# The fall-back verdict of a top-k attention kernel: carried to one SBUF row by a transfer instead of summed over the rows by a TensorE matmul

## The chip, the cores and the metric

The kernel runs on one core of one Trainium2 chip. The metric is the device time of one execution in microseconds (us), lower is better. TensorE (PE) multiplies matrices, VectorE (DVE), ScalarE (ACT) and GpSimd (POOL) work elementwise, SyncE (SP) issues all DMA transfers here. Each engine runs its own instructions in program order; engines wait for each other, and for transfers, on semaphores.

## The reference, cut to what matters

Input is one sequence of 2048 rows by 1024 columns in float32. Three layers follow each other: a mixture layer, the attention, and the same mixture layer again. The attention has 32 query heads over 8 key/value heads (four query heads share one), head size 32, and keeps for each query and head only the 204 largest causal scores:

```python
draft = jnp.einsum('bhqd,bhkd->bhqk', qr, kr)
draft = draft + jnp.where(causal_future, neg, jnp.asarray(0.0, dtype))
num_remain = max(min(Sq, MIN_REMAIN), Sq - int(Sq * MASK_OUT))
_, draft_indices = jax.lax.top_k(draft, num_remain)
mask = jnp.full((B, H, Sq, Sq), neg, dtype)
...
scores = jnp.einsum('bhqd,bhkd->bhqk', qr, kr) / np.sqrt(HD).astype(np.float32) + mask
attn = jax.nn.softmax(scores, axis=-1)
out = jnp.einsum('bhqk,bhkd->bhqd', attn, v)
```

## The kernel before, in words

Phase A (to about 828 us) does the first mixture layer and the projections, phase B (828 to 4199 us) the attention, phase C the rest. The change touches phase B alone.

Phase B goes through 128 **places** p. A place is one tile of 128 queries with one key/value group, so four heads. Groups 0, 2, 4, 6 take their tiles 0 to 15 upward, the odd groups 15 to 0 downward. Tile i sees 128*(i+1) keys, so a low tile is narrow and a high one wide. Tile 0 keeps all its keys and is not searched; 120 places are.

For a searched place the kernel looks for each query's threshold. PE computes the scores, DVE copies them to SBUF (`evacuate`, L1121), ACT counts by sign sums how many lie above a guess (L948), POOL improves the guess twice (`first_update`, `second_update`), DVE subtracts it (`difference`, L1129), finds the eight scores nearest to it (`nearest`, L1142, L1144) and picks the exact threshold from them (`choose`, result `dk`). DVE then writes the four masks (`masks`, L1259). PE multiplies keys by queries again with the masks added (`weights`, L834 to L840), ACT takes the exponential (L957), PE multiplies with the values (`values`, L868), turns the result back (`turn_back`, L878), and DVE normalises it (`normalise`, L1265, L1268).

The pick can fail where too many scores lie between guess and threshold. POOL's `judge` therefore makes `bad`, 128 queries by four heads in bf16, non-zero where it failed (L1082 is the last of its seven operations). PE's `flags` (L886) multiplies `bad` by a matrix of ones, which leaves in every row of four PSUM columns the sum over the 128 queries. DVE's `read_flag` (L1159) takes the maximum of the four columns into `flg`, and `fall_back` loads it into a register (L1167) and branches (L1168): if it is above zero, a slow exact search is run on DVE. In this input that happens in four places.

What sets the order: each engine's program is written out by a loop over j, with stages of several places in one turn. In turn j, DVE evacuates place j+2, searches place j (`directions`, `nearest`, `choose`), does `difference` of j+1, `normalise` of j-2, three of the four masks of j, `read_flag(j)`, the fourth mask, `fall_back(j)`, and a small memset (L1298) that counts up the semaphore `go`. PE does in turn j the weights of place j-1, and between them at fixed shares of the row the scores of j+2 and the first of j+3; `flags(j)` stands at the end of the row (share 1.0), or behind `turn_back(j-2)`. The first `weights` of place j in the next turn waits for `go`. POOL does in turn j `selectors(j)`, `second_update(j+1)`, `judge(j)`, `fold(j+1)`, `first_update(j+2)`. SP does in turn j `store(j-2)`, then seven transfers of queries for place j+4.

Of the kernel before, what the change touches and what calls it, by code (L numbers as in the profile page):

```python
# [17 lines left out]
ALU = mybir.AluOpType  # L18
ACT = mybir.ActivationFunctionType
AX = mybir.AxisListType  # L20
# [607 lines left out]
FLAGS = REP * VP  # L628
# [4 lines left out]
FLAG_AT, NEXT_R_AT = 1.0, 0.75  # L633


def phase_b(nc, b, dram):
# [12 lines left out]
    def searching(p):  # L649
        return here(p) and searched[p]  # L650
# [29 lines left out]
    def spread(events, n):  # L680

        at = [[] for _ in range(n + 1)]
        for f, e in events:
            at[math.ceil(f * n) if e[0] == "F" else int(f * n)].append(e)
        return at

    with ExitStack() as ctx:
# [28 lines left out]
        heads_bad = sb("heads_bad", [P, REP])  # L716
        rec = sb("rec", [P, REP])
# [12 lines left out]
        sm = semaphores(nc, ctx, "fill rs evac sign t1 t2 df sel key dk bad flagged flg mask go st ex pv ot otr norm mf "  # L730
# [4 lines left out]
        written = [ctx.enter_context(nc.semaphore(f"b_written{n}")) for n in range(2)]  # L735

# [9 lines left out]
        with nc.Block() as block:  # L746
            @block.sync
            def _(sp):
# [24 lines left out]

                def store(p):
# [11 lines left out]
                for j in range(N + 2):  # L786
                    if j >= 2:
                        store(j - 2)
# [10 lines left out]
            def _(pe):  # L799
# [71 lines left out]
                def turn_back(p):  # L871
# [3 lines left out]
                    if chosen[min(p + 2, N)]:  # L875
                        pe.wait_ge(sm["flg"], chosen[min(p + 2, N)])
# [14 lines left out]
                for j in range(-2, N + 2):  # L891
# [4 lines left out]
                    if searching(j):  # L896
                        events.append((FLAG_AT, ("F", j, 0)))
# [4 lines left out]
                    held = None  # L902
                    for n in range(len(todo) + 1):
                        for kind, p, h in at[n]:
                            if kind == "R":
                                scores(p, h)
                            elif back:
                                flags(p)
                            else:
                                held = p  # L910
# [11 lines left out]
                        if not back and seen == min(LAG + 2, blocks[p]):  # L922
                            turn_back(j - 2)
                            back = True
                            if held is not None:
                                flags(held)
# [72 lines left out]
            def _(pool):  # L999
# [72 lines left out]
                def judge(p):  # L1072
# [9 lines left out]
                    gp.tensor_tensor(bad[:, p % 2, :], c, far, ALU.add).then_inc(sm["bad"], 1)  # L1082
# [15 lines left out]
            def _(dve):  # L1098
# [58 lines left out]
                def read_flag(p):  # L1157
                    dve.wait_ge(sm["flagged"], chosen[p + 1])
                    v.tensor_scalar(heads_bad[:, :], psum[:, 7, FLAGS:FLAGS + REP], 0.0, None, ALU.add, ALU.max,  # L1159
                                    accum_out=flg[:, 0:1]).then_inc(sm["flg"], 1)  # L1160

                def fall_back(p):
# [5 lines left out]
                    with dve.If(any_bad > 0):  # L1168
# [6 lines left out]
                        then(v.tensor_scalar(heads_bad[:, :], heads_bad[:, :], 0.0, None, ALU.is_gt))  # L1175
                        then(v.tensor_reduce(several, heads_bad[:, :], AX.X, ALU.add))
                        then(v.tensor_tensor(heads_bad[:, :], heads_bad[:, :], b.steps[:, 0:REP], ALU.mult))
                        then(v.tensor_reduce(c, heads_bad[:, :], AX.X, ALU.max))
                        then(v.tensor_scalar(which, c, 0.5, None, ALU.subtract))
# [39 lines left out]
                        then(v.tensor_scalar(several, several, 1.5, None, ALU.is_gt))  # L1219
                        then(v.tensor_tensor(c[0:QUAD, :], c[0:QUAD, :], several[0:QUAD, :], ALU.max))  # L1220
# [128 lines left out]
```

## Time and profile before

| | |
|---|---|
| median of three runs | 4733.16 us (4732.83 to 4733.44) |
| the profiled execution: time, span | 4739.29 us, 4737.5 us |
| busy DVE, PE, ACT, POOL, share of the span | 67%, 74%, 57%, 43% |
| mean granted TensorE clock | 0.843 of full speed |
| packets of the DMA queue that SP fills, share of 16 DMA engines | 8.9% |

The span is the profiled execution from first to last instruction. A busy share is a mean over three unlike phases, so it does not say what holds up phase B; the waits do. A wait is put down to the instruction that released it last. For DVE, ACT and POOL the time in which an instruction only waits or branches is idle time of the engine.

### The profile page before, as it was taken

How to read it: one execution, taken by the hardware profiler on the slowest of the kernel's cores; microseconds unless marked ns; L12 is line 12 of the kernel's file. 1: busy time of each engine (PE TensorE's matmuls, PEld its weight loads, DVE VectorE, ACT ScalarE, POOL GpSimd, SP SyncE). 2: the span in 40 equal slices, each digit the busy share in tenths (PEclk: the TensorE clock that was granted, in tenths of full speed). 3: DMA queues.
4: the chain of work that ended last, by engine and by line, in shares of the span. 5: the costliest groups of instructions: out<-in, count | busy, mean ns of one | idle time of the engine just before them, and what ended most of it. 6: DMA issues, size and time to landing. Idle time of an engine off the chain costs nothing. (4 is left out here: it accounts for less than half of the span.)

```text
span 4737.5 us, 56552 instructions
## 1 busy us (share of the span) xinstructions
PE 3524.3 (74%) x16248; PEld 1649.4 (35%) x16248; DVE 3173.2 (67%) x6104; ACT 2688.0 (57%) x4577; POOL 2023.6 (43%) x5916
## 2 busy tenths in 40 slices
PE   5777775677868757787885678888567888857776
PEld 2333332233323323333332233333233333324443
DVE  2444444688988758888884888887488888822222
ACT  0111111688858757886885688887478888820000
POOL 1121211655535755554575554456565445620000
PEclk8777776688989878898997789989779999978887
DMA  2111111100001010000100100010010000011111
GB/s 97 42 52 43 51 40 44 34 11 11 9 6 21 16 30 12 11 9 7 21 16 19 24 11 9 9 21 14 19 26 11 9 9 11 15 72 53 54 40 40
DMA packets 221534, 124.04 MB, mean 26 GB/s; under 512 B 187940, under 2 KB 206628, under 8 KB 221092
## 3 DMA queue, kind: packets, MB, share of 16 engines
q1 hardware_dynamic: 221092, 119.36, 8.9%
q8 instruction: 130, 2.13, 0.2%
q14 instruction: 312, 2.56, 0.2%
HBM read 76.28 MB, written 42.99 MB: 25 GB/s over the span
## 5 line engine op out<-in xcount | busy, mean ns | idle before, releaser
L868 PE MATMUL banks<-pT,v_sb 128*65 128x512 f32 x2176 | 1186.3, 629 | 34.9 <-ACT oT L972 33.4
L957 ACT ACTIVATE pT<-banks 128x512 f32<-128x512 f32 x1088 | 637.7, 592 | 641.3 <-PE banks L840 634.9
L816 PE MATMUL banks<-k_sb,q_sb 128*128 128x512 bf16 (+3 forms) x1280 | 515.5, 403 | 388.5 <-DVE sc L1121 355.0
L1144 DVE MAX8 near<-keys 128x8 f32<-128x256 f32 (+14 forms) x480 | 653.4, 1361 | 16.5
L948 ACT ACTIVATE junk<-sc,t_all 128x256 fp8e4<-128x256 f32 (+14 forms) x480 | 599.2, 1249 | 31.9 <-DVE sc L1121 30.1
L948 ACT ACTIVATE junk<-sc,tiny 128x256 fp8e4<-128x256 f32 (+14 forms) x480 | 595.5, 1246 | 36.5 <-DVE sc L1129 36.2
L948 ACT ACTIVATE junk<-sc,tt 128x256 fp8e4<-128x256 f32 (+14 forms) x480 | 598.4, 1247 | 1.4 <-POOL tt L1013 0.8
L834 PE MATMUL banks<-q_sb,k_sb 128*128 128x512 bf16 x1088 | 447.0, 411 | 146.4 <-DVE fb L1298 124.7
L1121 DVE TENSOR_SCALAR_CACHE_REDUCE sc<-banks 128x1024 f32<-128x1024 f32 (+7 forms) x512 | 501.3, 980 | 52.1 <-PE banks L821 30.0
L1129 DVE TENSOR_SCALAR sc<-sc,tt 128x256 f32<-128x256 f32 (+14 forms) x480 | 360.5, 814 | 241.6 <-POOL tt L1034 241.5
L818 PE MATMUL banks<-k_sb,q_sb 96*128 96x512 bf16 (+3 forms) x1280 | 504.8, 404 | 0.0
L840 PEld LDWEIGHTS banks<-eye,mk 128*128 128x128 bf16 x4352 | 359.9, 103 | 301.2 <-issue 73.3
L840 PE MATMUL banks<-eye,mk 128*128 128x128 bf16 x4352 | 448.6, 228 | 0.0
L836 PE MATMUL banks<-q_sb,k_sb 99*128 99x512 bf16 x1088 | 444.9, 409 | 0.0
L1021 POOL TENSOR_SCALAR pw_b<-dd 128x4 f32<-128x4 f32 x120 | 31.8, 265 | 880.9 <-ACT junk L948 880.9
L1142 DVE TENSOR_SCALAR keys<-sc,flip 128x256 int32<-128x256 int32 (+14 forms) x480 | 393.0, 819 | 5.7 <-issue 1.4
L354 PE MATMUL banks<-wqkv,a_xT 128*128 128x512 f32 x768 | 376.1, 654 | 13.6 <-ACT a_xT L168 13.6
L816 PEld LDWEIGHTS banks<-k_sb,q_sb 128*128 128x128 bf16 x1280 | 138.4, 108 | 665.4 <-DVE sc L1121 455.9
L1259 DVE TENSOR_SCALAR mk<-sc,dk 128x256 bf16<-128x256 f32 (+14 forms) x480 | 369.5, 812 | 0.3 <-issue 0.3
L168 ACT ACTIVATE a_xT<-banks 128x512 f32<-128x512 f32 x64 | 34.7, 594 | 463.0 <-PE banks L148 463.0
L868 PEld LDWEIGHTS banks<-pT,v_sb 128*65 128x65 f32 x2176 | 228.7, 147 | 50.1 <-issue 38.7
L834 PEld LDWEIGHTS banks<-q_sb,k_sb 128*128 128x128 bf16 x1088 | 113.4, 104 | 380.2 <-DVE fb L1298 141.5
(247 smaller groups left out, 5469.8 us busy)
## 6 DMA issues: line engine op xcount, KB each, us to landing
q_sb<-scratch_qk SPq DMA_DIRECT2D x896, 32.0 KB, 1.9
scratch_qk<-parts SPq DMA_DIRECT2D x16, 960.0 KB, 3.7
a_x<-in_x SPq DMA_DIRECT2D x16, 512.0 KB, 3.2
scratch_x<-a_x SPq DMA_DIRECT2D x16, 512.0 KB, 2.6
scratch_attn<-o_sb SPq DMA_DIRECT2D x128, 64.0 KB, 1.6
c_xn<-scratch_attn SPq DMA_DIRECT2D x16, 512.0 KB, 3.6
c_x<-scratch_x SPq DMA_DIRECT2D x16, 512.0 KB, 4.5
out<-c_x SPq DMA_DIRECT2D x16, 512.0 KB, 2.6
```

Source lines behind the costliest of these rows:

```text
L354: last = nc.tensor.matmul(b.psum[:, 4 * (t % 2) + j, :], b.xT[:, t % U, c, :], wqkv[:, c, j * BANK:(j + 1) * BANK], start=(c == 0), stop=( ...
L816: nc.tensor.matmul(r_slot(n)[:, j:j + wj], q_sb[:, p % QS, 0, h, :], k_sb[:, group[p] % 2, 0, col:col + wj], start=True, stop=False)
L818: last = nc.tensor.matmul(r_slot(n)[:, j:j + wj], q_sb[0:K1, p % QS, 1, h, :], k_sb[0:K1, group[p] % 2, 1, col:col + wj], start=False, sto ...
L834: nc.tensor.matmul(psum[:, bank, :], k_sb[:, group[p] % 2, 0, cols], q_sb[:, p % QS, 0, :, :].rearrange("p h n -> p (h n)"), start=True, s ...
L836: nc.tensor.matmul(psum[:, bank, :], k_sb[0:ONES_AT + PARTS_OF_MAX, group[p] % 2, 1, cols], q_sb[0:ONES_AT + PARTS_OF_MAX, p % QS, 1, :, : ...
L840: last = nc.tensor.matmul(psum[:, bank, h * P:(h + 1) * P], mk[:, p % 2, h, cols], b.eye16[:, :], start=False, stop=(h == REP - 1))
L868: nc.tensor.matmul(psum[0:VP, 6, :], v_sb[:, group[p] % 2, kb, :], pT[:, n % PTS, :], start=(kb == 0), stop=(kb == blocks[p] - 1)).then_in ...
L948: nc.scalar.activation(junk[:, n % 2, 0:w], s, ACT.Sign, bias=bias, scale=scale, accum_out=into, saturate=False)\
L957: nc.scalar.activation(pT[:, tn % PTS, :], psum[:, 4 + n % 2, :], ACT.Exp, scale=SCALE)\
L1121: v.tensor_scalar(sc[:, p % SCS, h, c * CHUNK:c * CHUNK + w], r_slot(n)[:, 0:w], 0.0, mx[:, p % 4, 0, h:h + 1] if c else None, ALU.add, AL ...
L1142: link(v.tensor_scalar(z.bitcast(I32), sc[:, p % SCS, h, 0:width[p]].bitcast(I32), 2, flip[:, h:h + 1], ALU.logical_shift_right, ALU.bitwi ...
L1144: v.max(near[:, h, :], z).then_inc(sm["key"], 1)
```

## The change

Five things are changed. PE's `flags` goes, with its place in PE's order and with the wait of `turn_back` on `flg`. SP gets `carry_verdict(j)` as the first thing of turn j: it waits for `bad` and moves the 128x4 bf16 values from 128 SBUF rows into one row of 512 elements (`verdict`, two slots in turn). `read_flag(j)` waits for that transfer's semaphore (`carried`) and takes the maximum over 512 SBUF elements of one row, in place of four PSUM columns. `fall_back` works out which heads failed from `verdict` when the branch is taken, with one more reduction. POOL waits with its next write into the same slot of `bad` until the slot has been carried.

```diff
+                def carry_verdict(p):
+                    sp.wait_ge(sm["bad"], chosen[p + 1])
+                    if p >= 2:
+                        sp.wait_ge(sm["go"], p - 1)
+                    sp.dma_start(verdict[0:1, chosen[p] % 2, :, :], bad[:, chosen[p] % 2, :]).then_inc(carried[chosen[p] % 2], 16)
...
                 for j in range(N + 2):
+                    if searching(j):
+                        carry_verdict(j)
                     if j >= 2:
                         store(j - 2)
...
-                    if chosen[min(p + 2, N)]:
-                        pe.wait_ge(sm["flg"], chosen[min(p + 2, N)])
...
-                def flags(p):
-                    pe.wait_ge(sm["bad"], chosen[p + 1])
-                    if p >= 2:
-                        pe.wait_ge(sm["norm"], p - 1)
-                    nc.tensor.matmul(psum[:, 7, FLAGS:FLAGS + REP], b.ones16[:, :], bad[:, p % 2, :],
-                                     start=True, stop=True).then_inc(sm["flagged"], 1)
...
-                    gp.tensor_tensor(bad[:, p % 2, :], c, far, ALU.add).then_inc(sm["bad"], 1)
+                    if chosen[p] >= 2:
+                        pool.wait_ge(carried[chosen[p] % 2], 16 * (chosen[p] // 2))
+                    gp.tensor_tensor(bad[:, chosen[p] % 2, :], c, far, ALU.add).then_inc(sm["bad"], 1)
...
                 def read_flag(p):
-                    dve.wait_ge(sm["flagged"], chosen[p + 1])
-                    v.tensor_scalar(heads_bad[:, :], psum[:, 7, FLAGS:FLAGS + REP], 0.0, None, ALU.add, ALU.max,
-                                    accum_out=flg[:, 0:1]).then_inc(sm["flg"], 1)
+                    dve.wait_ge(carried[chosen[p] % 2], 16 * (chosen[p] // 2 + 1))
+                    if chosen[p]:
+                        dve.wait_ge(sm["flg"], chosen[p])
+                    v.tensor_scalar(passed[:, :], verdict[:, chosen[p] % 2, :, :].rearrange("o q h -> o (q h)"), 0.0, None,
+                                    ALU.add, ALU.max, accum_out=flg[0:1, 0:1]).then_inc(sm["flg"], 1)
...
-                        then(v.tensor_scalar(heads_bad[:, :], heads_bad[:, :], 0.0, None, ALU.is_gt))
+                        then(v.tensor_reduce(heads_bad[0:1, :], verdict[:, chosen[p] % 2, :, :].rearrange("o q h -> o h q"),
+                                             AX.X, ALU.max))
+                        then(v.tensor_scalar(heads_bad[0:1, :], heads_bad[0:1, :], 0.0, None, ALU.is_gt))
```

How the order on the engines moves is shown at place 36 (group 2, tile 4). On PE, before, at the end of its turn; the names after the arrow are the inputs, L878 turns back place 34, L816 to L821 are scores of place 39, L834 is the first `weights` of place 36:

```order
L868 MATMUL banks<-pT,v_sb 65x512 [waits b_ot,b_ex]
L878 MATMUL banks<-eye,oT 128x65 [waits b_flg,b_norm,b_ot]
L878 MATMUL banks<-eye,oT 128x65 x3
L886 MATMUL banks<-bad,ones 128x4 [waits b_norm,b_bad]
L816 MATMUL banks<-k_sb,q_sb 128x512 [waits b_evac]
L818 MATMUL banks<-k_sb,q_sb 128x512
L816 MATMUL banks<-k_sb,q_sb 128x512
L818 MATMUL banks<-k_sb,q_sb 128x512
L821 MATMUL banks<-future,eye 128x128
L834 MATMUL banks<-q_sb,k_sb 128x512 [waits b_ex,b_go]
```

On PE, now, at the same place; where the changed file's lines L826 to L844 are L816 to L834 before, L878 is L868, and L886 is L878:

```order
L878 MATMUL banks<-pT,v_sb 65x512 [waits b_ot,b_ex]
L886 MATMUL banks<-eye,oT 128x65 [waits b_norm,b_ot]
L886 MATMUL banks<-eye,oT 128x65 x3
L826 MATMUL banks<-k_sb,q_sb 128x512 [waits b_evac]
L828 MATMUL banks<-k_sb,q_sb 128x512
L826 MATMUL banks<-k_sb,q_sb 128x512
L828 MATMUL banks<-k_sb,q_sb 128x512
L831 MATMUL banks<-future,eye 128x128
L844 MATMUL banks<-q_sb,k_sb 128x512 [waits b_ex,b_go]
```

The matmul on `bad` is gone and nothing else has moved; the scores of place 39 no longer stand behind a wait for `bad`, and the `weights` still stand behind `go`.

On DVE, before, around `read_flag` of place 36:

```order
L1268 TENSOR_TENSOR o_sb<-banks,rec 128x128 [waits b_written0,b_vchain]
L1259 TENSOR_SCALAR mk<-sc,dk 128x640 [waits b_dk,b_st]
L1259 TENSOR_SCALAR mk<-sc,dk 128x640 x2
L1159 TENSOR_SCALAR heads_bad,flg<-banks 128x4 [waits b_flagged]
L1259 TENSOR_SCALAR mk<-sc,dk 128x640
L1167 TENSOR_LOAD flg [waits b_flg]
```

On DVE, now, the same place:

```order
L1265 TENSOR_TENSOR o_sb<-banks,rec 128x128 [waits b_written0,b_vchain]
L1256 TENSOR_SCALAR mk<-sc,dk 128x640 [waits b_dk,b_st]
L1256 TENSOR_SCALAR mk<-sc,dk 128x640 x2
L1154 TENSOR_SCALAR passed,flg<-verdict 1x512 [waits b_flg,b_carried1]
L1256 TENSOR_SCALAR mk<-sc,dk 128x640
L1162 TENSOR_LOAD flg [waits b_flg]
```

The place in the order is the same; the wait is now for a transfer, and the fourth mask, the load of the flag and `go` stand behind it as before.

On SP, now, two turns (L780 is the new transfer, L784 the store, L756 the loads of queries; before, the rows were the same without L780):

```order
L780 DMA verdict<-bad 1x128x4 [waits b_go,b_bad]
L784 DMA scratch_attn<-o_sb 128x128 [waits b_norm]
L756 DMA q_sb<-scratch_qk 32x4x128 [waits b_st]
L756 DMA q_sb<-scratch_qk 32x4x128 x6
L780 DMA verdict<-bad 1x128x4 [waits b_go,b_bad]
```

Store and loads of a turn now stand behind the wait for that turn's `bad`.

## Rows read from the trace of the kernel before

**Rows 1.** Windows: phase B; us, busy (instructions) of each engine, clock, DMA.

```profile
828.00:4199.00 3371.00, 2567.82 (x12902) 1134.11 (x12903) 2683.80 (x4980) 2529.36 (x4221) 1855.89 (x5448) 0.87 0.07 15
```

**Rows 2.** Waits of DVE: who for whom, us in total, times, longest.

```profile
DVE sc L1129 <- POOL tt L1034: 241.5, 84, 12.7
...
DVE dirn L1133 <- ACT junk L948: 149.8, 57, 4.8
...
DVE fb L1298 <- issue: 50.1, 20, 3.4
```

**Rows 3.** Waits of PE.

```profile
PE banks L886 <- POOL bad L1082: 237.1, 97, 7.1
...
PE banks L834 <- DVE fb L1298: 124.7, 58, 22.6
```

**Rows 4.** Timeline, place 36 (tile 4): start, us, instruction, [idle before <-releaser].

```profile
1773.75 0.49 POOL L1082 TENSOR_TENSOR bad<-gp,js 128x4 bf16<-128x4 f32 x1
...
1775.03 0.15 DVE L1159 TENSOR_SCALAR_CACHE_REDUCE heads_bad<-banks 128x4 f32<-128x4 f32 x1
...
1778.96 0.61 PE L834 MATMUL banks<-q_sb,k_sb 128*128 128x512 bf16 x1 [2.65 <-DVE fb L1298]
```

**Rows 5.** Timeline, place 47 (tile 15).

```profile
2119.89 1.12 POOL L1082 TENSOR_TENSOR bad<-gp,js 128x4 bf16<-128x4 f32 x1
...
2122.06 0.15 DVE L1159 TENSOR_SCALAR_CACHE_REDUCE heads_bad<-banks 128x4 f32<-128x4 f32 x1
```

**Rows 6.** Source lines: ns min/median/max, first and last start.

```profile
L1082 POOL TENSOR_TENSOR bad<-gp,js x120: 201/735/1218, 861.5 to 4187.2; 128x4 bf16<-128x4 f32 x120
```

**Rows 7.** Source line of `read_flag`.

```profile
L1159 DVE TENSOR_SCALAR_CACHE_REDUCE heads_bad<-banks x120: 144/152/163, 862.0 to 4189.3; 128x4 f32<-128x4 f32 x120
```

**Rows 8.** DMA issues: count, KB each, median us from issue to landing.

```profile
q_sb<-scratch_qk SPq DMA_DIRECT2D x896, 32.0 KB, 1.9
...
scratch_attn<-o_sb SPq DMA_DIRECT2D x128, 64.0 KB, 1.6
...
tab_a<-in_tab SPq DMA_DIRECT2D x16, 3.5 KB, 2.8
```

**Rows 9.** Groups of DVE by form: count, busy us, mean ns.

```profile
L1121 DVE TENSOR_SCALAR_CACHE_REDUCE sc<-banks 128x512 f32<-128x512 f32 x32 | 21.8, 680 | 3.7 <-PE banks L821 3.3
...
L1259 DVE TENSOR_SCALAR mk<-sc,dk 128x512 bf16<-128x512 f32 x32 | 14.0, 478 | 0.0
```

**Rows 10.** Timeline of `go` (L1298): ends of places 84, 85, 93, 116 and 125.

```profile
3159.97 0.06 DVE L1298 MEMSET fb<- 128x1 f32 x1 [0.30 <-DVE mk L1259]
...
3192.55 0.06 DVE L1298 MEMSET fb<- 128x1 f32 x1 [2.76 <-issue]
...
3364.07 0.06 DVE L1298 MEMSET fb<- 128x1 f32 x1 [3.40 <-issue]
...
3988.78 0.06 DVE L1298 MEMSET fb<- 128x1 f32 x1 [0.28 <-DVE mk L1259]
...
4180.43 0.06 DVE L1298 MEMSET fb<- 128x1 f32 x1
```

**Rows 11.** The same line at the ends of places 9, 10, 13, 73 and 77.

```profile
1042.06 0.06 DVE L1298 MEMSET fb<- 128x1 f32 x1 [0.42 <-DVE mk L1259]
...
1076.12 0.06 DVE L1298 MEMSET fb<- 128x1 f32 x1 [2.84 <-issue]
...
1177.75 0.06 DVE L1298 MEMSET fb<- 128x1 f32 x1
...
2769.19 0.06 DVE L1298 MEMSET fb<- 128x1 f32 x1 [0.43 <-DVE mk L1259]
...
2903.51 0.06 DVE L1298 MEMSET fb<- 128x1 f32 x1 [0.16 <-DVE mk L1259]
```

**Rows 12.** Timeline, first `weights` behind the end of place 24.

```profile
1573.89 0.39 PE L834 MATMUL banks<-q_sb,k_sb 128*128 128x512 bf16 x1 [1.81 <-DVE fb L1298]
```

**Rows 13.** The page's costliest groups: busy us, mean ns, idle before and releaser.

```profile
L1121 DVE TENSOR_SCALAR_CACHE_REDUCE sc<-banks 128x1024 f32<-128x1024 f32 (+7 forms) x512 | 501.3, 980 | 52.1 <-PE banks L821 30.0
```

More of the change, by code:

```diff
@@ L627 @@
 K_ROWS = ((0, 1, 0, 1), (2, 0, 2))
-FLAGS = REP * VP
 QUAD = 32
@@ L632 @@
 R_AT = (0.06, 0.25, 0.42)
-FLAG_AT, NEXT_R_AT = 1.0, 0.75
+NEXT_R_AT = 0.75
 def phase_b(nc, b, dram):
@@ L683, in spread @@
         for f, e in events:
-            at[math.ceil(f * n) if e[0] == "F" else int(f * n)].append(e)
+            at[int(f * n)].append(e)
         return at
@@ L716, in phase_b @@
         heads_bad = sb("heads_bad", [P, REP])
+        verdict = sb("verdict", [1, 2, P, REP], BF16)
+        passed = sb("passed", [1, P * REP], BF16)
         rec = sb("rec", [P, REP])
@@ L728, in phase_b @@
         psum = b.psum
-        sm = semaphores(nc, ctx, "fill rs evac sign t1 t2 df sel key dk bad flagged flg mask go st ex pv ot otr norm mf "
+        sm = semaphores(nc, ctx, "fill rs evac sign t1 t2 df sel key dk bad flg mask go st ex pv ot otr norm mf "
                         "vchain pchain", "b")
@@ L735, in phase_b @@
         written = [ctx.enter_context(nc.semaphore(f"b_written{n}")) for n in range(2)]
+        carried = [ctx.enter_context(nc.semaphore(f"b_carried{n}")) for n in range(2)]
         def r_slot(n):
@@ L901, in _ @@
                     seen, back = 0, not here(j - 2)
-                    held = None
                     for n in range(len(todo) + 1):
                         for kind, p, h in at[n]:
[L905 to L910, printed above, removed]
+                            scores(p, h)
                         if n == len(todo):
@@ L924, in _ @@
                             back = True
-                            if held is not None:
-                                flags(held)
                     if j == N:
@@ L1174, in fall_back @@
                         dve.drain()
-                        then(v.tensor_scalar(heads_bad[:, :], heads_bad[:, :], 0.0, None, ALU.is_gt))
[L1176 to L1179, printed above, removed]
+                        then(v.tensor_reduce(heads_bad[0:1, :], verdict[:, chosen[p] % 2, :, :].rearrange("o q h -> o h q"),
+                                             AX.X, ALU.max))
+                        then(v.tensor_scalar(heads_bad[0:1, :], heads_bad[0:1, :], 0.0, None, ALU.is_gt))
+                        then(v.tensor_reduce(several[0:1, :], heads_bad[0:1, :], AX.X, ALU.add))
+                        then(v.tensor_tensor(heads_bad[0:1, :], heads_bad[0:1, :], b.steps[0:1, 0:REP], ALU.mult))
+                        then(v.tensor_reduce(c[0:1, :], heads_bad[0:1, :], AX.X, ALU.max))
+                        then(v.tensor_scalar(which[0:1, :], c[0:1, :], 0.5, None, ALU.subtract))
                         hb = dve.value_load(fbi[0:1, 7:8], min_val=0, max_val=REP - 1)
@@ L1218, in fall_back @@
                         then(v.tensor_reduce(c[0:QUAD, :], quads[0:QUAD, :], AX.X, ALU.max))
-                        then(v.tensor_scalar(several, several, 1.5, None, ALU.is_gt))
-                        then(v.tensor_tensor(c[0:QUAD, :], c[0:QUAD, :], several[0:QUAD, :], ALU.max))
+                        then(v.tensor_scalar(several[0:1, :], several[0:1, :], 1.5, None, ALU.is_gt))
+                        then(v.tensor_tensor(c[0:1, :], c[0:1, :], several[0:1, :], ALU.max))
                         still = dve.value_load(fb[0:1, 0:1].bitcast(I32), min_val=0, max_val=FLAG_BITS)
```

4 lines of the change are left out of this document (1 added, 3 removed).

## The prediction, made before the changed kernel had run

> **What bounds the kernel now.** I read the windows first, then the waits, then the timeline of single turns. Phase B takes 3371 of the 4737.5 us, and DVE is busy for 2684 us of it, 80%, ACT 75%, PE 76% [rows 1]. No engine is full, so the turn is a ring and not one engine's work. The waits show the ring. DVE waits 241.5 us for POOL's second guess, which waits for ACT's counts, and 149.8 us for ACT directly [rows 2]. ACT's counts stand in its program between exponentials, and those wait for PE's `weights`, whose first one waits for `go` (124.7 us in 58 turns) [rows 3]. And `go` is DVE's last act of the turn. So the ring is: DVE's masks, `read_flag`, fourth mask, `go`; PE `weights`; ACT; POOL; DVE. `read_flag` lies on it, before `go`. The largest wait that the change removes, PE's 237.1 us for `bad` in 97 turns [rows 3], lies beside it: behind `flags` PE has only scores to do before it waits for `go` anyway.
>
> **How long a verdict may take.** In place 36 `bad` ends at 1773.75 + 0.49 = 1774.24 and `read_flag` starts at 1775.03: 0.79 us [rows 4]. In place 47 it is 2122.06 - 2121.01 = 1.05 us [rows 5]. Pairing all 120 `bad` with their `read_flag`, first 861.5 with 862.0, last 4187.2 with 4189.3 [rows 6, 7], the slack is 1.06 us on average in the 80 places of tiles 1 to 10 and 1.26 in the 40 of tiles 11 to 15. PE's detour through `flags` fits in it almost everywhere.
>
> **The transfer.** It is new, so I bound it by the nearest rows. SP is idle when `bad` comes: its seven loads of the turn before are issued long before (the shortest turns are near 8 us, the loads take 3.5). From issue to landing the store, 128 packets, takes 1.6 us, a query load with SBUF as its target, also 128 packets, 1.9, and the smallest transfer there is, 3.5 KB in packets of 28 bytes behind a large load, 2.8 [rows 8]. To this comes about 0.1 us for SP's and DVE's wake-up (SP starts the store 0.03 us after its release in the turns I looked at, and a landing is followed 0.05 us later). So 1.6 us at best (the store's packets are 512 bytes, 8-byte ones save at most 0.1), 2.95 at worst. I take 1.9, between store and load, nearer to the load for its SBUF target. Against the slack, place by place, 1.9 us is late by 69 us in the narrow 80 places (76 of them late) and by 29 us in the wide 40 (35 late).
>
> The Trainium skill, "DMA: Bandwidth & Descriptors", section "Anatomy of one DMA — SWDGE (gpsimd) path", says that most of a small transfer's fixed cost is the receipt of the write, heaviest for HBM. By that rule the SBUF target should land before the store's 1.6 us; the rows say the reverse (1.9 into SBUF), though the loads also queue behind each other, so I leave the sum as it is.
>
> **The longer maximum.** `read_flag` now goes over 512 elements instead of 4, which took 152 ns [rows 7]. The same operation on 512 PSUM elements takes 680 ns, a plain one from SBUF on 512 elements 478 ns [rows 9]. So it grows by 0.33 to 0.53 us; if bf16 in and out went twice as fast again as the plain one, by some 0.2. I take 0.5, since the accumulating form is the same operation: 120 x 0.5 = 60 us, 40 in the narrow places and 20 in the wide. Fewer rows save nothing, since a DVE operation works on all rows at once.
>
> The Trainium skill, "SBUF — State Buffer", in its list of practical consequences for the shared port pair, says that `tensor_scalar` can enter the two-port modes, but not in the form that also writes its accumulator; "VectorE: DVE Perf Modes", section "The perf-mode tier table", gives bf16 `tensor_scalar` four elements a cycle. By the first rule the growth is the 0.5 us taken; by the second alone it would be an estimated 0.13 us, and the whole sum 37 us less. The rows agree with the first as far as they go, since 680 ns for 512 elements is one element at a time.
>
> **What of a delay reaches the end.** The trace holds its own experiment. In 20 turns DVE loses about 2.4 us more than usual between the flag's load and `go`, at exactly this place, waiting for no other engine (50.1 us under "issue") [rows 2]. Group 5 has five such turns in places 85 to 93 (first 2.76, last 3.40 us of idle time); group 7 has the same widths in places 117 to 125 and none. From `go` to `go` the one takes 3364.07 - 3159.97 = 204.1 us, the other 4180.43 - 3988.78 = 191.7: 12.4 us for 5 x 2.4 = 12.0 [rows 10]. In tiles 1 to 10 a delay before `go` arrives whole. In wide turns ACT's own chain of counts competes. Places 10 to 13 with one delay (2.84 instead of 0.42) take 135.7 us, places 74 to 77 without take 134.3: 1.4 of 2.4 [rows 11]. Two more such pairs (places 110 to 112 against 46 to 48, 78 to 80 against the same) give 0.3 and 2.2, so I take half.
>
> **The sum.** Narrow: 69 + 40 = 109, all of it. Wide: (29 + 20) / 2 = 24.5. The fall-backs, four in this input, get one reduction over 512 elements each, which at the rate of the 680 ns operation is 0.7 us: 3. Removed: the flag's matmul and its load of weights, 0.3 us in a turn on an engine that then waits for `go`: 0. The wait of `turn_back` on `flg` was for the verdict of the turn before: 0. POOL's new wait is for a transfer of two searches ago: 0. SP's store and seven loads start about 0.8 us later in the turn; the queries are wanted a turn later, and the places whose loads land just in time (35, 36 and their like) follow turns without a verdict: 0, or 0.5 us a group if I am wrong. Together 109 + 24.5 + 3 = 137 us. On the profiled execution's 4739.3 us that makes 4876; it lies 6 us above the median of the runs, so against 4733.2 I forecast 4870.
>
> Two costs have no row of their own. The "issue" delays may fall on more or fewer turns, since DVE's code shifts: 2.4 us each, some 20 us either way if half of them change. And PE's idle stretch before its first `weights` grows by over 1 us. After 2.65 us of idle time this matmul takes 0.61 us (the 1.2 GHz level), against 0.39 after 1.81 us of idle time (the 2.4 GHz level) [rows 4, 12]; a few more turns at the lower level would cost up to 10 us.
>
> **The rivals.**
> 1. *The waits swallow it.* DVE has 391 us of waits for POOL and ACT [rows 2] against a raw delay of 98 + 60 = 158 us. If those waits shrank by what is lost before `go`, half or all of it would vanish: 4812 for half everywhere, 4736 for all of it. For it speaks only the size of the waits; against it the 12.4 of 12.0 us. Half or so everywhere 15%, nearly all 3%.
> 2. *The transfer is slow*, 2.95 us, because 128 eight-byte writes go into one row. Late by 151 us in the narrow and 67 in the wide places: 151 + 40 + (67 + 20) / 2 + 3 = 238, so 4971. For it speaks the small-packet load's 2.8 us; against it that this one queues behind 512 KB. 15%, with 2.3 us and more counted to it.
> 3. *Faster: PE, freed from `bad`, runs ahead.* PE no longer stands up to 7.1 us before scores it could do [rows 3]. Where the next place is one chunk wide they come earlier, and DVE, which sits idle for 52.1 us in all before it copies scores [rows 13], could save up to that: 4681, if the transfer cost nothing. It decides from the point where a verdict lands and is read within the slack of 1.1 us, and even the best row, 1.6, is beyond. 2%.
> 4. *The form I predict*, a transfer of 1.7 to 2.3 us, arriving whole in narrow turns: 65%.
>
> **How the numbers follow.** The likeliest gives 4870. Its best corner, 1.6 us and 0.2 us of growth, with half in the wide places, is 46 + 16 + (19 + 8) / 2 + 3 = 79, so 4812; with the waits swallowing some of that, 4795. The upper side is cut between this case and rival 2, at 4950. The measurement tells apart 0.2%, 9.5 us. Slower by more: 94%; within it: 4%; faster: 2%.
>
> **What would show it.** DVE's wait at `read_flag`, next to nothing before, should now be a wait for the DMA of about 0.8 us in 110 or so turns, near 95 us in total. The operation should last 0.65 us, and issue to landing of the verdict 1.8 us. PE's wait for `go` should grow by roughly what its wait for `bad` loses, the waits on L1129 and L1133 should shrink in the wide turns only, and narrow turns should be 1.3 us longer each. If DVE's wait is there and turns are not longer, rival 1 holds; if it is above 1.5 us a turn, rival 2.

## The result, and the profile after

The changed kernel takes 4888.66 us, median of four runs (4884.45 to 4897.99), against 4733.3 us for the kernel before in the same comparison: a ratio of 1.0331, 95% interval 1.0313 to 1.0349, or 155 us more. Forecast were 4870 us in a range of 4795 to 4950. The two profiled executions lie closer together, 4884.45 and 4739.29 us (145 us apart), since the one of before is above its median and the one of after is the lowest of its four.

The windows view, phase B of the changed kernel, columns as in [rows 1]:

```profile
825.00:4346.00 3521.00, 2519.47 (x12544) 1131.61 (x12784) 2757.40 (x4984) 2531.84 (x4221) 1879.00 (x5448) 0.85 0.07 14
```

Against [rows 1] phase B is 150 us longer, and this is all of the difference. DVE is busy 74 us more, ACT 2 us more. The granted clock is 0.85 instead of 0.87. The rest of the 150 us is idle time of DVE.

The waits of DVE, changed kernel:

```profile
DVE sc L1122 <- POOL tt L1025: 260.1, 86, 13.1
...
DVE dirn L1126 <- ACT junk L939: 94.7, 46, 4.9
DVE passed L1154 <- DMA verdict<-bad: 91.8, 105, 1.8
...
DVE fb L1295 <- issue: 69.4, 27, 3.3
```

The third row is the new wait, 91.8 us in 105 turns. The second answers to 149.8 us in [rows 2] and has lost 55 us: ACT's counts are ready earlier relative to a DVE that comes later. Added up turn by turn, this wait fell from 107.8 to 73.9 us in the wide turns, but also from 42.1 to 20.8 in the narrow ones. The wait for POOL, the largest, has not shrunk (241.5 before), and grew by 15.5 us in the narrow turns. The last row grew from 50.1 us in 20 turns to 69.4 in 27, which no term of the sum holds.

The waits of PE:

```profile
PE banks L826 <- DVE sc L1114: 435.6, 94, 23.6
PE banks L844 <- DVE fb L1295: 247.8, 39, 24.5
PE banks L846 <- DVE fb L1295: 134.3, 19, 13.2
```

The 237.1 us for `bad` [rows 3] are gone. The waits for `go` went from 124.7 to 382.1 us (both rows), which is 257 us more for the 237 that are gone, and those for DVE's evacuation are now 435.6. PE does its scores sooner and then stands before `go` for longer. Behind it ACT stands too, for PE before its exponentials: 775.0 us, against 634.9 in the trace of before.

The turn of place 36 on the timeline, the one of [rows 4]:

```profile
1813.15 1.47 DVE L1256 TENSOR_SCALAR mk<-sc,dk 128x640 bf16<-128x640 f32 x3
1813.26 0.49 POOL L1075 TENSOR_TENSOR bad<-gp,js 128x4 bf16<-128x4 f32 x1
...
1813.77 0.48 SPq L780 DMA_DIRECT2D verdict<-bad  x1
...
1814.30 0.59 SPq L784 DMA_DIRECT2D scratch_attn<-o_sb  x1
...
1815.67 0.67 DVE L1154 TENSOR_SCALAR_CACHE_REDUCE passed<-verdict 1x512 bf16<-1x512 bf16 x1 [1.06 <-DMA verdict<-bad]
...
1816.29 0.07 DVE L1154 DVE_READ_ACCUMULATOR passed<-verdict 1x1 f32 x1
1816.29 0.54 DVE L1256 TENSOR_SCALAR mk<-sc,dk 128x640 bf16<-128x640 f32 x1
...
1817.59 0.06 DVE L1295 MEMSET fb<- 128x1 f32 x1 [0.76 <-DVE mk L1256]
1817.70 0.10 PEld L844 LDWEIGHTS banks<-q_sb,k_sb 128*128 128x128 bf16 x1 [8.45 <-DVE fb L1295]
...
1817.70 0.61 PE L844 MATMUL banks<-q_sb,k_sb 128*128 128x512 bf16 x1 [8.12 <-DVE fb L1295]
```

`bad` ends at 1813.75 and the read starts at 1815.67: 1.92 us, where the kernel before took 0.79. Of them SP's start is 0.02, the issue 0.48, the way to the landing 1.40, DVE's start 0.02. Three masks end at 1814.62, and DVE stands still for 1.06 us. The fourth mask cannot fill this: it is behind the waiting instruction.

Source lines of the new transfer and of the new read, all 120 of each:

```profile
DMA to landing us min/median/max: 1.9/1.9/2.3
...
L1154 DVE TENSOR_SCALAR_CACHE_REDUCE passed<-verdict x120: 666/674/675, 860.9 to 4335.4; 1x512 bf16<-1x512 bf16 x120
```

The operation takes 674 ns on one row, where 152 ns stood for four elements on 128 rows [rows 7].

`go` on the timeline at the ends of places 84, 93, 116 and 125, as in [rows 10]:

```profile
3243.13 0.06 DVE L1295 MEMSET fb<- 128x1 f32 x1 [0.30 <-DVE mk L1256]
...
3458.70 0.06 DVE L1295 MEMSET fb<- 128x1 f32 x1 [3.19 <-issue]
...
4110.03 0.06 DVE L1295 MEMSET fb<- 128x1 f32 x1 [0.32 <-DVE mk L1256]
...
4325.40 0.06 DVE L1295 MEMSET fb<- 128x1 f32 x1
```

Places 85 to 93 take 215.6 us instead of 204.1: 11.5 more for nine narrow turns, with five "issue" delays in both kernels. Places 117 to 125 take 215.4 instead of 191.7: 23.7 more, and here the changed kernel has four such delays where there were none. They are 11.9 us of idle time together, where the same four turns had 2.3 before, so 9.6 more; the remaining 14.1 us are 1.6 a turn. Places 21 to 29, without a delay in either, took 12.9 more, 1.4 a turn.

Over all of phase B, tile by tile, the changed kernel needs 127.5 us more in the 80 narrow turns and 20.4 in the 40 wide ones. Put against what DVE lost:

| us | wait at the read | longer operation | more "issue" delay | raw | arrived |
|---|---|---|---|---|---|
| narrow | 65.5 | 41.8 | 23.1 | 130.4 | 127.5 |
| wide | 26.3 | 20.9 | 5.5 | 52.7 | 20.4 |

The wait and the longer operation lie before `go`. Of the third column 14.2 and 5.1 us do; the rest are delays at other instructions of DVE, behind `go`. These are sums over one execution each. Of the runs below, two whose time is all but that of the kernel before are shorter than it in the narrow turns of such an execution, b_carry_only by 7.0 us and b_pad by 9.4, so a share of these 130 us is good to somewhat under a tenth.

The page's part 5 has the group that answers to [rows 13]:

```profile
L1114 DVE TENSOR_SCALAR_CACHE_REDUCE sc<-banks 128x1024 f32<-128x1024 f32 (+7 forms) x512 | 501.1, 980 | 53.6 <-PE banks L831 28.4
```

DVE's idle time before it copies scores is 53.6 us, against 52.1. That PE no longer waits for `bad` bought nothing here.

### The profile page after: what moved, and what is told of

Read it like the earlier page. It is cut to its first block and busy times, and to the rows that moved or that the text cites. A ratio compares the mean times of both kernels' runs of the same rounds, so it can differ in the third digit from the quotient of the medians.

```text
span 4881.9 us, 56438 instructions
## 1 busy us (share of the span) xinstructions
PE 3471.1 (71%) x15889; PEld 1644.7 (34%) x16128; DVE 3246.7 (67%) x6108; ACT 2690.4 (55%) x4577; POOL 2046.0 (42%) x5916
## 5 line engine op out<-in xcount | busy, mean ns | idle before, releaser
L878 PE MATMUL banks<-pT,v_sb 128*65 128x512 f32 x2176 | 1194.7, 633 | 33.4 <-ACT oT L963 31.8
L948 ACT ACTIVATE pT<-banks 128x512 f32<-128x512 f32 x1088 | 638.7, 592 | 781.9 <-PE banks L850 775.0
L826 PE MATMUL banks<-k_sb,q_sb 128*128 128x512 bf16 (+3 forms) x1197 | 472.9, 395 | 470.2 <-DVE sc L1114 435.6
L844 PE MATMUL banks<-q_sb,k_sb 128*128 128x512 bf16 x932 | 382.3, 410 | 264.8 <-DVE fb L1295 247.8
L1114 DVE TENSOR_SCALAR_CACHE_REDUCE sc<-banks 128x1024 f32<-128x1024 f32 (+7 forms) x512 | 501.1, 980 | 53.6 <-PE banks L831 28.4
L826 PEld LDWEIGHTS banks<-k_sb,q_sb 128*128 128x128 bf16 x1280 | 137.1, 107 | 862.0 <-DVE sc L1114 637.5
L844 PEld LDWEIGHTS banks<-q_sb,k_sb 128*128 128x128 bf16 x1088 | 113.9, 105 | 627.8 <-DVE fb L1295 394.8
L878 PEld LDWEIGHTS banks<-pT,v_sb 128*65 128x65 f32 x2176 | 230.3, 148 | 49.7 <-issue 38.8
```

What stands on the lines that cost most here:

```text
L826: nc.tensor.matmul(r_slot(n)[:, j:j + wj], q_sb[:, p % QS, 0, h, :], k_sb[:, group[p] % 2, 0, col:col + wj], start=True, stop=False)
L844: nc.tensor.matmul(psum[:, bank, :], k_sb[:, group[p] % 2, 0, cols], q_sb[:, p % QS, 0, :, :].rearrange("p h n -> p (h n)"), start=True, s ...
L878: nc.tensor.matmul(psum[0:VP, 6, :], v_sb[:, group[p] % 2, kb, :], pT[:, n % PTS, :], start=(kb == 0), stop=(kb == blocks[p] - 1)).then_in ...
L948: nc.scalar.activation(pT[:, tn % PTS, :], psum[:, 4 + n % 2, :], ACT.Exp, scale=SCALE)\
L1114: v.tensor_scalar(sc[:, p % SCS, h, c * CHUNK:c * CHUNK + w], r_slot(n)[:, 0:w], 0.0, mx[:, p % 4, 0, h:h + 1] if c else None, ALU.add, AL ...
```

## The experiments

The names are those of the expectations. Edits are against the kernel before, or, where the name begins with a, against the changed one.

**The transfer alone (b_carry_only).** The kernel before, with SP's transfer added, nobody waiting for it before the end, and PE's `flags` kept. `bad` takes its slot by the count of searches, as in the changed kernel.

```diff
+                    if searching(j):
+                        carry_verdict(j)
...
+                    if chosen[p] >= 2:
+                        pool.wait_ge(carried[chosen[p] % 2], 16 * (chosen[p] // 2))
...
+                    sp.wait_ge(carried[n], 16 * (chosen[N] // 2))
```

> The kernel before, with the transfer of bad into the verdict row added at the head of SP's turn, but nothing on DVE waits for it and the flag matmul stays. Theory A (the loss is DVE's wait for the transfer, 92 us, and the longer maximum, 62 us, both standing before go): no change, within 0.2% of 4733 us. Rival B (SP's queue: the store and the seven query loads of each turn start later and that holds PE up): a good part of the 155 us, over 40 us.

Measured: 4739.14 us against 4733.88, 1.0011 (1.0002 to 1.0021), 5 us, near the edge of what can be told. So SP's longer turn, POOL's wait and the later store and loads cost next to nothing, as the prediction had it; rival B, over 40 us, is out. Twelve of the 120 transfers landed late, 2.2 to 3.55 us after their issue, and nothing waited for them.

**The wait alone (b_carry_wait).** As the last, and `read_flag` waits for the transfer as well as for PE; its operation stays the short one.

```diff
                     dve.wait_ge(sm["flagged"], chosen[p + 1])
+                    dve.wait_ge(carried[chosen[p] % 2], 16 * (chosen[p] // 2 + 1))
```

> The same, and DVE's read_flag also waits for the transfer before it takes its four PSUM columns; the flag matmul and the short maximum stay. Theory A: the wait of about 92 us in all, 65 in tiles 1 to 10 whole and 27 in tiles 11 to 15 at the measured 0.4, so +76 us, 4809 us (4795 to 4825). Rival C (it is the removed matmul, by a longer idle stretch of PE at the lower clock, that costs a large part): clearly less than 76, under 50 us, since the matmul is still there.

Measured: 4868.63, 1.0286 (1.0267 to 1.0305): 135 us where 76 were expected. A miss by 59 us, and the waits of DVE in it show most of it:

```profile
DVE heads_bad L1173 <- DMA verdict<-bad: 113.7, 106, 3.2
...
DVE fb L1312 <- issue: 67.7, 29, 3.5
...
DVE heads_bad L1173 <- PE banks L897: 8.7, 7, 1.8
```

The wait itself is 22 us longer than in the changed kernel. With two waits in a row before the read there are 0.116 us between landing and read instead of 0.024, about 10 us in all. Eleven transfers land 2.7 to 3.6 us after their issue and one at 2.06, together 14.6 us above the usual 1.88; in the changed kernel four are above 2.0, by 1.0 us together. One of the eleven in the DMA view of 2536 to 2541 us:

```profile
q8 instruction: 1, 0.02, 1.6%
issues: line engine op xcount, KB each, median us to landing
q_sb<-scratch_qk SPq DMA_DIRECT2D x3, 32.0 KB, 2.0
scratch_attn<-o_sb SPq DMA_DIRECT2D x1, 64.0 KB, 3.1
verdict<-bad SPq DMA_DIRECT2D x1, 1.0 KB, 3.4
```

One packet of 16 KB of instructions occupies a DMA engine for 1.26 us from 2538.58 on, and the verdict that was issued at 2537.61 lands 3.4 us after that. In all eleven such a 16 KB packet starts between issue and landing, and of the other 109 in one. And the "issue" delays before `go` grew from 50.1 to 67.7 us. In narrow turns 113.6 us arrived. What this run shows is therefore the direction only: the wait costs with the short operation too, and with the flag matmul still there, so rival C (under 50 us) is out. Its size holds things that the changed kernel does not have.

**The longer operation alone (b_long_op).** The kernel before with the changed kernel's operation ahead of its own, on a `verdict` that is always zero and needs no wait.

```diff
                     dve.wait_ge(sm["flagged"], chosen[p + 1])
+                    if chosen[p]:
+                        dve.wait_ge(sm["flg"], chosen[p])
+                    v.tensor_scalar(passed[:, :], verdict[:, :], 0.0, None, ALU.add, ALU.max, accum_out=fake[0:1, 0:1])
```

> The kernel before with one further DVE operation in read_flag, a maximum over 512 bf16 elements of one row that holds zeros (0.67 us and what its accumulator read adds), its result unused. Nothing is waited for. Theory A: 120 x 0.67 = 80 us on DVE, 54 whole and 27 at 0.4, so +65 us, 4798 us (4785 to 4815). Rival D (an operation on one row hides behind DVE's other waits): under 30 us.

Measured: 4821.74, 1.0187 (1.0169 to 1.0204), 88 us where 65 were expected. The operation took its 667 ns; what was missing in the expectation is in the waits again:

```profile
DVE fb L1305 <- issue: 71.6, 28, 3.4
```

That is 21 us more "issue" than before. Narrow turns took 71.2 us more, wide ones 8.6. Rival D, under 30 us, is out. An estimate of what the changed kernel's growth costs by itself (0.52 us a turn instead of this run's 0.75): with some 20 us taken off for the delays, (88 - 20) x 0.52 / 0.75 = 47 us, where the prediction's term arrives as 40 + 10 = 50.

**The verdict one search late (a_late).** The changed kernel, but DVE reads the verdict of the search before, which has long landed. It leaves out the fall-back where it is needed and runs it a turn later. The operation and the transfer are the same, without the wait; SP issues the transfer only behind `go` of the place before.

```diff
-                        sp.wait_ge(sm["go"], p - 1)
+                        sp.wait_ge(sm["go"], p)
...
-                    dve.wait_ge(carried[chosen[p] % 2], 16 * (chosen[p] // 2 + 1))
+                    old = max(chosen[p] - 1, 0)
+                    dve.wait_ge(carried[old % 2], 16 * (old // 2 + 1))
...
-                    v.tensor_scalar(passed[:, :], verdict[:, chosen[p] % 2, :, :].rearrange("o q h -> o (q h)"), 0.0, None,
+                    v.tensor_scalar(passed[:, :], verdict[:, old % 2, :, :].rearrange("o q h -> o (q h)"), 0.0, None,
```

> The changed kernel, but read_flag and fall_back take the verdict of the search before, carried a turn earlier; so the fall-back runs one search late, on scores that do not need it, and as often. The transfer, the 512-element maximum and the missing matmul stay, and DVE's wait goes. Theory A: 4889 - 76 = 4813 us (4795 to 4825), and no wait of DVE for the verdict in the trace. Rival B or C: stays above 4850 us.

Measured: 4814.72, 1.0172 (1.0153 to 1.019), a hit within 2 us. The waits of DVE:

```profile
DVE fb L1297 <- issue: 67.9, 26, 3.5
...
DVE passed L1156 <- DMA verdict<-bad: 1.8, 1, 1.8
```

The wait has shrunk from 91.8 to 1.8 us, and 74 of the 155 us are gone. In the profiled executions the narrow turns took 65.9 us more than before instead of 127.5, so 61.6 came back for 63.7 us of wait, and the wide ones 6.2 instead of 20.4, so 14.2 for 26.3. The "issue" delays stayed, so in the changed kernel they don't come from the wait. This is the cleanest measure of the transfer's price, and it splits the loss: 74 us for waiting, 81 for the operation, the "issue" delays and the rest.

**Half as many elements (a_int32).** The changed kernel reads the 512 bf16 values as 256 int32.

```diff
-                    v.tensor_scalar(passed[:, :], verdict[:, chosen[p] % 2, :, :].rearrange("o q h -> o (q h)"), 0.0, None,
-                                    ALU.add, ALU.max, accum_out=flg[0:1, 0:1]).then_inc(sm["flg"], 1)
+                    v.tensor_scalar(passed[:, :], verdict[:, chosen[p] % 2, :, :].rearrange("o q h -> o (q h)").bitcast(I32), 2.0 ** -24, None,
+                                    ALU.mult, ALU.max, accum_out=flg[0:1, 0:1]).then_inc(sm["flg"], 1)
```

> The changed kernel with the verdict row read as 256 int32 instead of 512 bf16 elements (a pair of bf16 is non-zero as an integer when either half is), scaled by 2 to the -24; the branch is taken as often. Theory A: the operation falls from 0.67 to about 0.41 us, 120 x 0.26 = 32 us on DVE, 21 of it in tiles 1 to 10 whole and 10 in the wide ones at 0.3, so 24 us less than the changed kernel, 4865 us (4855 to 4875). Rival D (the length of the operation does not count, only the wait): 4880 to 4895.

Measured: 4866.31, 1.0284 (1.027 to 1.0298), expected 4865. Its source line:

```profile
L1154 DVE TENSOR_SCALAR_CACHE_REDUCE passed<-verdict x120: 399/406/408, 860.8 to 4315.4; 1x256 f32<-1x256 int32 x120
```

Against the 152 ns for four elements [rows 7] 256 int32 elements took 254 ns more, 1.01 ns each, and 512 bf16 elements 522 more, 1.03 each: the time follows the count of elements, and not their bytes. 120 x 0.268 = 32 us were taken from the operation and 23 came back.

**The read one mask earlier (b_early).** No transfer. In the kernel before, `read_flag` moves ahead of the third mask for tiles 2 to 10.

```diff
-                        if searching(j) and h + 1 == REP:
+                        if searching(j) and h + (2 if 2 <= tile_of[j] <= 10 else 1) == REP:
```

> The kernel before, its flag matmul kept, with read_flag one mask earlier on DVE in tiles 2 to 10: two masks instead of one then cover the load of the flag and the branch. Theory A (a microsecond before go in a narrow turn is a microsecond of time): the idle time before go, 0.4 to 0.9 us in those turns, shrinks by a mask's 0.35 to 0.8 where PE's verdict is there in time, some 0.35 us in 72 turns: 25 us less, 4708 us (4695 to 4720). Rival E (the verdict is late by as much, as DVE now comes 0.3 to 0.8 us earlier and PE's detour takes 0.3): 4728 to 4745.

Measured: 4706.07 against 4732.77, 0.9943 (0.9929 to 0.9956), expected 4708. It is 27 us faster than the kernel before and so the fastest of all here. The end of the turn of place 37 in it, and in the kernel before:

```profile
1835.45 0.15 DVE L1159 TENSOR_SCALAR_CACHE_REDUCE heads_bad<-banks 128x4 f32<-128x4 f32 x1
1835.53 0.08 DVE L1159 DVE_READ_ACCUMULATOR heads_bad<-banks 128x1 f32 x1
1835.53 1.41 DVE L1259 TENSOR_SCALAR mk<-sc,dk 128x1024 bf16<-128x1024 f32 x2
1837.01 0.06 DVE L1298 MEMSET fb<- 128x1 f32 x1
```

```profile
1851.87 0.15 DVE L1159 TENSOR_SCALAR_CACHE_REDUCE heads_bad<-banks 128x4 f32<-128x4 f32 x1
1851.94 0.08 DVE L1159 DVE_READ_ACCUMULATOR heads_bad<-banks 128x1 f32 x1
1851.94 0.75 DVE L1259 TENSOR_SCALAR mk<-sc,dk 128x1024 bf16<-128x1024 f32 x1
1853.26 0.06 DVE L1298 MEMSET fb<- 128x1 f32 x1 [0.56 <-DVE mk L1259]
```

From the end of the read (1852.02) to `go` are 1.24 us (1.20 or more in all 120 turns): between them lie the load of `flg` into a register and the branch over the body. One mask covers 0.75 of it, two cover 1.41, and the 0.56 us of idle time is gone. It is the ring of the prediction from the other side: in narrow turns DVE's idle time before `go` falls from 80.0 to 46.3 us, its wait at the read grows by 2.5, and 34.1 us arrive for these 31.2. The limit is the slack: at the read DVE now waits 8.7 us for PE, in 13 turns, where it was 4.7 in 4. One of them, place 25, shows PE's way bare:

```profile
1583.14 0.52 POOL L1082 TENSOR_TENSOR bad<-gp,js 128x4 bf16<-128x4 f32 x1
...
1583.72 0.18 PE L886 MATMUL banks<-bad,ones 128*128 128x4 bf16 x1 [2.06 <-POOL bad L1082]
...
1583.93 0.16 DVE L1159 TENSOR_SCALAR_CACHE_REDUCE heads_bad<-banks 128x4 f32<-128x4 f32 x1 [0.33 <-PE banks L886]
```

`bad` ends at 1583.66, and 0.27 us later DVE reads the sum. At places 36 and 47 the sum was there 0.24 us after `bad`; the 0.79 and 1.05 us of [rows 4] and [rows 5] are DVE's time, which came to the read that late. PE's way is longer where PE is still busy with something else: over 0.3 us in 23 of the 120 turns of the kernel before.

**PE freed from `bad` (b_late_flags).** The kernel before, `flags` multiplies the `bad` of the search before. It leaves out the fall-back where it is needed and runs it a turn late.

```diff
-                    pe.wait_ge(sm["bad"], chosen[p + 1])
+                    old = max([q for q in range(p) if searched[q]], default=p)
+                    pe.wait_ge(sm["bad"], chosen[old + 1])
+                    if chosen[p]:
+                        pe.wait_ge(sm["flg"], chosen[p])
...
-                    nc.tensor.matmul(psum[:, 7, FLAGS:FLAGS + REP], b.ones16[:, :], bad[:, p % 2, :],
+                    nc.tensor.matmul(psum[:, 7, FLAGS:FLAGS + REP], b.ones16[:, :], bad[:, old % 2, :],
```

> The kernel before, but PE's flags multiplies the bad of the search before, so PE never waits for POOL's bad; the fall-back runs one search late, as often. Theory A (that wait lies beside the ring): PE's 237 us of waits for bad go, its waits for go and for evacuations grow by as much, and the time stays within 0.3% of before, 4720 to 4745. Rival F (PE freed of the wait runs ahead and DVE's 52 us of waits for scores shrink): 4680 to 4715.

Measured: 4740.78, 1.002 (1.0011 to 1.0029), 8 us slower and within the expected 4720 to 4745. The waits of PE:

```profile
PE banks L816 <- DVE sc L1124: 407.4, 124, 22.8
PE banks L889 <- DVE o_sb L1271: 172.0, 67, 6.4
PE banks L834 <- DVE fb L1301: 131.8, 58, 5.4
```

The wait for `bad` is gone, but `flags` also waits for `normalise`, so PE still stood 172.0 of the 237.1 us, and what it saved it spent waiting for DVE (407.4 against 355.0). It tests rival 3 only in part. DVE's wait for scores did not shrink (30.1 us, against 30.0 in [rows 13]). In the changed kernel and in a_late PE's wait for `bad` is gone altogether. In a_late DVE lost 41.2 us in narrow turns by the operation, 24.1 by "issue" delays and 1.8 by waiting, 67.1 together, and 65.9 arrived: nothing beyond the noise is left for PE's freedom. No run takes the whole wait away and nothing else.

**Where the "issue" delays come from (b_pad, b_wait_pad, b_pad5).** Three edits of the kernel before that ask for no work. b_pad puts one more operation, with the drain behind it, into `fall_back`'s body, which is skipped in all but four turns; b_wait_pad adds a wait that is always satisfied at `read_flag`; b_pad5 puts five copies of b_pad's operation into the body.

```diff
+                        then(v.tensor_scalar(badq[:, 1:2], heads_bad[:, 0:1], 0.0, None, ALU.mult))
                         then(v.tensor_scalar(heads_bad[:, :], heads_bad[:, :], 0.0, None, ALU.is_gt))
```

```diff
                     dve.wait_ge(sm["flagged"], chosen[p + 1])
+                    if chosen[p]:
+                        dve.wait_ge(sm["flg"], chosen[p])
```

> The kernel before with one further instruction in the body of the fall-back branch, which runs in four turns of 120; in the other 116 only the later code of DVE lies one instruction further on in each turn. Every kernel so far in which DVE's code grew shows 67 to 72 us of issue waits before go in 26 to 29 turns, before has 50.1 in 20. Theory S (where DVE's code lies decides in how many turns it waits for code behind the branch): 65 to 72 us of issue waits and 10 to 20 us more, 4743 to 4753. Rival T (those waits come from the longer operation or the wait before them): unchanged, 4733 to 4736.

> The kernel before, read_flag also waiting on flg of the search before, which is always there: one further wait instruction that DVE runs in every turn, and no operation and no transfer. Theory S2 (an instruction that is run in each turn, not one in the skipped body, moves DVE onto more turns with a late code load, 22 instead of 15): 65 to 72 us of issue waits before go, 4743 to 4753. Theory S3 (how many turns wait for code is a matter of where the code happens to lie, and any small shift draws anew): 12 to 24 such turns, 4725 to 4755, and no rule. Rival T (they come with a longer stay of DVE in front of the branch, by an operation or a wait of its own): 15 to 17 turns, 4730 to 4740.

> The kernel before with five further instructions (each with its drain) in the skipped body of the branch in place of one. Theory S3: again 12 to 24 turns with a late code load, not near the 17 of one instruction by any rule, 4725 to 4755. Rival U (a longer body makes more turns wait for code, since the branch jumps over more of it): 20 turns or more, 4743 to 4760. Rival T: 15 to 17 turns, 4730 to 4740.

Measured, in this order: 4733.96 us, 1.0005 (0.9996 to 1.0014); 4740.98, 1.0019 (1.001 to 1.0027); and 4770.05, 1.0078 (1.0065 to 1.0091), with these waits of DVE, one kernel each:

```profile
DVE fb L1299 <- issue: 55.0, 23, 3.4
```

```profile
DVE fb L1300 <- issue: 52.8, 22, 3.3
```

```profile
DVE fb L1303 <- issue: 82.0, 32, 3.3
```

Before it was 50.1 us in 20 turns [rows 2]. One operation in the body or one wait outside did next to nothing, against theories S and S2: the long delays, over 1.5 us, are 17 in either, against 15 before. b_pad's time is rival T's, and b_wait_pad's lies within S3 and 1 us above T. Five gave 32 us more in 32 turns, against S3 and T; rival U's 20 turns or more holds, but its 4743 to 4760 us was too low. So a longer skipped body does make more turns late, and b_pad5 is slower by 37 us, although its operations are run in four turns only. (In its profiled execution, the fastest of its six, phase B is 23 us longer.)

How often is one half of it, where the other. The long delays fall on the same 15 places in the kernel before, in b_early and in b_carry_only, whose code for DVE is as long in every turn (10, 34, 36, 38, 43, 50, 62, 78, 85, 87, 89, 91, 93, 106, 111). b_wait_pad has 17 at others; b_carry_wait, which also has one wait more a turn, has all of these 17 and five further ones. The changed kernel has 22 long ones and b_long_op 23, and 21 places are the same. So it looks as if the length of DVE's code picks the places, and with the same length a kernel whose DVE waits for a transfer had five more. Against the kernel before, the changed one has b_pad's growth of the body and b_wait_pad's extra wait together. No run has just these two.

## Why the prediction was right, step by step

**The bound.** The ring through `read_flag` and `go` was read rightly. Of 130.4 us that DVE lost in narrow turns, 121.5 of them before `go`, 127.5 arrived, and for 31.2 us taken away there 34.1 came back (b_early).

**The transfer.** Taken at 1.9 us from `bad` to the read, measured 1.93. That the nearest row, the query load, fitted so well is partly luck: it moves 32 KB from HBM, the verdict 1 KB inside SBUF, and nothing before the run tied the two. The wait was to be near 95 us in 110 or so turns; it is 91.8 in 105. The store's 1.6 would have been wrong, and so would the 2.95 of rival 2. The slack was there too, but as DVE's lateness: PE's own way took 0.27 us where DVE stood waiting for it (b_early, place 25).

The Trainium skill, "DMA: Bandwidth & Descriptors", section "Anatomy of one DMA — SWDGE (gpsimd) path", calls the receipt of the write heaviest for HBM. The earlier landing in SBUF that the prediction drew from it did not come: from issue to landing the verdict took 1.88 us, the store of 64 KB to HBM 1.6 before, and from the end of the issue 1.40 against 1.24 to 1.28. These times hold more than the receipt, and both go by SP's queue, so no run here shows the receipt itself.

**The longer maximum.** Taken as 0.5 us of growth and an operation of 0.65, measured 0.52 and 0.674: 62.6 us against 60. The rule of "SBUF — State Buffer" in the Trainium skill, that the form with an accumulator does not enter the two-port modes, agrees: 1.03 ns for each bf16 element, no faster than the int32 ones with 1.01. By the tier table of "VectorE: DVE Perf Modes" in the Trainium skill alone the sum would have been an estimated 37 us lower. The fall-backs' reduction, 3 us in the sum, took four times 674 ns.

**Whole in narrow turns, half in wide.** Narrow: 0.98 of the raw delay. Wide: 0.39, where half was taken, from three pairs of turns that gave 0.3 to 2.2 of 2.4 us; that it came so near is luck in part. The share is not one number: 14.2 of 26.3 us for the wait (a_late) and 8.6 of some 35 for the added operation and its delays (b_long_op). In the wide turns DVE's wait for ACT took up what did not arrive: it fell by 33.9 us, and 32.3 are missing. One sign failed here. The waits for ACT and POOL were to shrink in wide turns only, but the one for ACT also fell by 21.3 us in the narrow ones. The one for POOL grew there by 15.5, so together they gave back 5.8, and the delay still arrived nearly whole. Rival 1 falls with the narrow turns.

**What was put at nothing.** PE's freedom: nothing (DVE's idle time before the scores 53.6 against 52.1 us, and the sum for a_late above). SP's and POOL's part: b_carry_only gives 5 us, where 0 to a little was foreseen. Here the store's issue takes 0.59 us, against 0.34 in the kernel before, and its landing 1.8 instead of 1.6.

**Where the size was off.** The sum was 137 us; phase B of the profiled execution is 149.6 longer, the medians lie 155 apart. The term that was mis-sized is the one without a row, the "issue" delays: given as 20 us either way and put at zero, they are 28.6 us more over all of DVE's waits in phase B (62.2 to 90.8), 23.1 of them in narrow turns. The prediction allowed for them, but had no ground for their sign. Against it stand the wide turns (20.4 instead of 24.5) and the wait (91.8 instead of 98). The clock term, up to 10 us, is there in kind: the granted clock fell from 0.87 to 0.85, and the first `weights` of a turn took the 0.61 us of the lower level in 114 turns instead of 99. That is 15 x 0.22 = 3 us for these matmuls; what others cost no run separates.

**How the parts add up.** The wait alone gave 135 us, the operation alone 88, together 155. The difference of 68 has these parts: the operation alone was an added one, not a replaced one (0.23 us a turn, some 20 us); the wait alone had the second wait before the read, the late transfers and 4 us more of waiting for PE, about 27; and both had the full growth of the "issue" delays, which the changed kernel has once, some 20. These are read off the traces, not tested singly.

**Open.** How many of the changed kernel's further late turns come from the longer body, how many from the extra wait, and why b_carry_wait has five more long ones than b_wait_pad. Why 16 KB packets start beside 11 or 12 transfers in b_carry_only and b_carry_wait, and beside none in the changed kernel.

## What to carry to other kernels

Before a wait on the ring is replaced, compare the way from producer to consumer with the slack at that place, turn by turn: a PE detour of 0.27 us, as in most turns here, fits into 1.06, a transfer of 1.93 does not, however few bytes it carries. In this kernel's narrow turns a delay on the ring arrived whole although the engines had hundreds of us of other waits, and a long wait beside the ring (237 us of PE) was worth nothing that could be measured. The question that paid was another one, what covers the chain read, load, branch, `go`: reading one mask earlier gave 0.6% for a one-line edit.

## What was not expected of the hardware

- Each long "issue" delay before `go` (over 1.5 us, 15 turns before, 22 after) has a packet of 8192 bytes on the instruction queue that starts 1.8 to 2.0 us before `go`; the whole execution has some 320 of them. At place 36 of the kernel before, DVE's idle time is 3.19 us, and the DMA view of 1775 to 1778 us shows the instruction queue at work:

```profile
q14 instruction: 2, 0.02, 2.0%
```

  So it looks as if DVE waits for its code there, behind the branch over the skipped body; whose instructions a packet holds the trace does not tell. Each such delay costs about 2.4 us, and a longer body gave more of them (b_pad5).
- Packets of 16 KB of instructions delayed small transfers: all 11 that took over 2.3 us in b_carry_only, and all 11 in b_carry_wait, had one start between issue and landing, and took 2.7 to 3.6 us instead of 1.9.
- The 1 KB transfer of 128 pieces of 8 bytes holds SP's queue for 0.48 us, and the 64 KB store behind it for 0.59.
- A reduction over one row cost DVE as much as one over 128 rows: 674 ns for 512 bf16 elements of one row in SBUF, 680 ns for 512 float32 elements of 128 rows in PSUM [rows 9].
